# Windowed attention and a routed FFN on one core: the order of work within a pass of the first half is changed

## What is computed

```python
scores = einsum('bhts,...', q, k) * scale          # q, k, v = split(x @ W_attn + b_attn)
scores = where(causal & (j >= i - 64), scores, -inf)
x = layernorm(x + softmax(scores) @ v @ W_proj + b_proj)
expert = argmax(softmax(x @ Wr.T))                  # one of 8 for each row
y = gelu(x @ W1[expert] + b1[expert]) @ Wo + bo + x
out = layernorm(x + layernorm(y) * gamma + beta)
```

## Time and profile before

| | us |
|---|---|
| three timed runs | 616.62, 617.55, 620.0 (median 617.55) |
| the profiled execution, its own time | 610.88 |
| its span, first to last instruction | 609.0 |
| first half, about | 0 to 360 of the span |

### The profile page before, as it was taken

One profiled execution on the slowest core, in us unless ns is written; L12 is line 12 of the kernel. 1 busy time (PEld: TensorE's weight loads), 2 busy tenths in 40 slices (PEclk: granted clock), 3 DMA queues, 4 the chain that ended last, 5 costly groups with the idle time before them and its releaser, 6 DMA issues. The chain is left out here.

```text
span 609.0 us, 29717 instructions
## 1 busy us (share of the span) xinstructions
PE 525.7 (86%) x11019; PEld 446.3 (73%) x11019; DVE 444.0 (73%) x1229; ACT 374.5 (62%) x843; POOL 311.3 (51%) x570
## 2 busy tenths in 40 slices
PE   3589889898899999989997843999999999999990
PEld 2557667777677777768776632999999999998870
DVE  4336776787777778777878867678888898886543
ACT  2875755767576675746576631776667666675450
POOL 7501333343434444343434541388888888886433
PEclk9958988999999999998999985999999999999986
DMA  7695976686576667674668102133322222221100
GB/s 192 156 213 141 232 226 175 169 205 167 145 192 192 174 169 190 168 198 129 185 153 212 64 21 60 46 90 98 98 80 72 81 72 72 72 81 47 32 9 6
DMA packets 94908, 77.46 MB, mean 127 GB/s; under 512 B 37030, under 2 KB 88367, under 8 KB 94770
## 3 DMA queue, kind: packets, MB, share of 16 engines
q1 hardware_dynamic: 91410, 67.12, 42.4%
q0 software_dynamic: 3264, 8.41, 3.9%
q10 hardware_dynamic: 96, 0.04, 0.0%
HBM read 43.63 MB, written 23.62 MB: 110 GB/s over the span
## 5 line engine op out<-in xcount | busy, mean ns | idle before, releaser
L1384 PE MATMUL ps<-v_even,w_hi 128*128 128x128 f16 (+1 forms) x1280 | 170.5, 216 | 1.5 <-DVE qs L1081 0.6
L1384 PE MATMUL ps<-v_even,w_lo 128*128 128x128 f16 (+1 forms) x640 | 132.1, 215 | 0.1
L838 ACT ACTIVATE probs<-ps,b1T 128x128 f32<-128x128 f32 (+1 forms) x320 | 87.3, 361 | 72.0 <-PE ps L1384 44.0
L1366 PE MATMUL ps<-wo_hi,ks 128*128 128x256 f16 x576 | 129.2, 274 | 1.0 <-DVE ks L1074 1.0
L1384 PEld LDWEIGHTS ps<-v_even,w_hi 128*128 x1280 | 120.8, 99 | 6.2 <-issue 2.8
L886 DVE TENSOR_REDUCE mx<-ps 128x4 bf16<-128x512 f32 x128 | 82.3, 684 | 2.4 <-PE ps L1171 2.0
L666 POOL CAST attT_hi<-att 128x256 f16<-128x256 f32 x32 | 12.7, 396 | 134.9 <-DVE att L955 134.9
L739 ACT ACTIVATE qs<-ps 32x1024 f16<-32x1024 bf16 x64 | 61.3, 1004 | 30.7 <-PE ps L1259 30.7
L1366 PE MATMUL ps<-wo_lo,ks 128*128 128x256 f16 x288 | 78.9, 274 | 0.0
L733 ACT ACTIVATE probs<-ps 128x512 f32<-128x512 f32 x128 | 73.7, 610 | 4.9 <-PE ps L1193 4.2
L1074 DVE TENSOR_TENSOR ks<-probs,ks 128x512 f16<-128x512 f32 x72 | 61.5, 855 | 19.2 <-ACT ks L845 19.2
(11 more groups left out here) (221 smaller groups left out, 1341.7 us busy)
## 6 DMA issues: line engine op xcount, KB each, us to landing
qk_s<-qk_hi SPq DMA_DIRECT2D x64, 128.0 KB
w_in<-in_L_ffn_W_dram SPq DMA_DIRECT2D x32, 256.0 KB, 4.9
v_odd<-slots SPq DMA_DIRECT2D x64, 128.0 KB, 2.1
qs<-qk_s SPq DMA_DIRECT2D x16, 384.0 KB
ks<-qk_s SPq DMA_DIRECT2D x16, 384.0 KB
v_even<-v_odd SPq DMA_DIRECT2D x63, 96.0 KB, 2.6
ks<-qk_s SPq DMA_DIRECT2D x32, 144.0 KB
qk_s<-qk_lo SPq DMA_DIRECT2D x32, 128.0 KB
```

What stands on the lines that cost most here:

```text
L838: last = nc.scalar.activation(g[1 - p][:, ic, n * width:(n + 1) * width], ps_h[1 - p][:, half, col + n * width:col + (n + 1) * width], ACT ...
L1366: ins = mm(ps_y[p], h[p][hs][:, ic, :], wo[ws][:, ic, :], start=n == 0, stop=n == 3 * IC - 1)
L1384: up_ins = mm(ps_h[1 - p][:, half, col + m * width:col + (m + 1) * width], weights(ws, owners[m], k, ic), sT[1 - p][ss][:, k, at], start=k ...
```

## The change

Only the order is changed, in the first half, and one small PSUM tile moves.

- ScalarE: the copy of the inverses (`rdenT`, L790) goes between `maxima_rows(0)` and `maxima_rows(1)`; `exps(1)` goes behind the high part of q and k.
- TensorE: q and k are now (0, 1), the inverses, (2, 3), all ahead of `scores_t`. The ranks go between `scores_t` 1 and 2. `values(0)` goes between `scores` 0 and 1.
- VectorE: `att` goes ahead of the low part of W1, place and slot ahead of the low part of q and k.
- SP: the W1 load goes behind the x load and is that of the next tile (n = it + 1). It waits for `w1l_done` of tile it-1, which VectorE gives in pass `it`.
- `ps_rank` goes from bank 7 to bank 1; waits follow it (`place_done` now ahead of the projection, `v_out` and `lx_done` ahead of the ranks).

```diff
-        ps_rank = ps[:, 7, C:C + 2 * E].rearrange("p (a e) -> p a e", a=2)
+        ps_rank = ps[:, 1, 320:320 + 2 * E].rearrange("p (a e) -> p a e", a=2)
@@ SP
-                n = it
-                if a_tile(n):
-                    cols = slice(n % 2 * I // 2, (n % 2 + 1) * I // 2)
-                    wait(sp, w1l_done, n - 1)
-                    sp.dma_start(w1_in[:, cols], w1_units[n // 2][:, cols]).then_inc(w1_ld[n % 2], 16)
                 n = it + LEAD + 2
...
                     sp.dma_start(xin[n % XRING], x_rows[n]).then_inc(xin_ld[n % 3], 16)
+                n = it + 1
+                if a_tile(n):
+                    cols = slice(n % 2 * I // 2, (n % 2 + 1) * I // 2)
+                    wait(sp, w1l_done, n - 1)
+                    sp.dma_start(w1_in[:, cols], w1_units[n // 2][:, cols]).then_inc(w1_ld[n % 2], 16)
@@ ScalarE
                     maxima_rows(0)
-                    maxima_rows(1)
-                if cur:
-                    exps(0)
                 n = it - 1
                 if a_tile(n):
...
                     nc.scalar.activation(rdenT[:, :, :], ps_rden, ACT.Copy).then_inc(rdenT_out, 1)
                 if cur:
-                    exps(1)
+                    maxima_rows(1)
+                    exps(0)
...
+                if cur:
+                    exps(1)
                 if a_tile(old):
                     act.wait_ge(y_done, old + 1)
@@ VectorE
                 if a_tile(done):
+                    dve.wait_ge(rdenT_out, done + 1)
+                    wait(dve, al_done, done)
+                    nc.vector.tensor_tensor(att[:, :, :], ps_num, rdenT[:, :, :], ALU.mult).then_inc(att_done, 1)
+                if a_tile(done):
                     piece, cols = done // 2, slice(done % 2 * I // 2, (done % 2 + 1) * I // 2)
...
+                if a_tile(new):      # behind place and slot
+                    dve.wait_ge(qkh_done, new + 1)
@@ TensorE
                 scores(0)
+                values(0)
                 scores(1)
-                values(0)
                 if a_tile(old):
...
+                    wait(pe, place_done, old)
...
-                queries_keys((0, 1, 2))
+                queries_keys((0, 1))
                 if a_tile(done):
                     pe.wait_ge(rdenp_done, done + 1)
-                    wait(pe, place_done, old)
...
-                if it < 0:
-                    queries_keys((3,))
+                queries_keys((2, 3))
...
                 scores_t(1)
-                if it >= 0:
-                    queries_keys((3,))
+                if a_tile(old):
+                    pe.wait_ge(onehot_done, old + 1)
+                    pe.wait_ge(v_out, upto(it + 1))
+                    pe.wait_ge(lx_done, upto(it + 1))
+                    mm(ps_rank[:, 0, :], before[:, :], onehot[:, :], start=True, stop=True)
+                    mm(ps_rank[:, 1, :], ones_b[:, :], onehot[:, :], start=True, stop=True).then_inc(rank_done, 1)
                 scores_t(2)
                 scores_t(3)
```

More of the change, by code:

```diff
@@ L951, in _ @@
                         .then_inc(w1l_done, 1)
[L952 to L963, removed]
                 if a_tile(old):
@@ L976, in _ @@
                     nc.vector.tensor_reduce(slot_of[old % 2][:, :], placed[:, :], AX.X, ALU.max).then_inc(slot_done, 1)
+                if a_tile(new):
+                    dve.wait_ge(qkh_done, new + 1)
+                    wait(dve, qk_st[new // 2 % 2], 16 * QK_STORES * (new // 4))
+                    hi, lo = (qk[new // 2 % 2][s][:, :, :, new % 2 * P:new % 2 * P + P].rearrange("p w m t -> p (w m) t")
+                              for s in range(2))
+                    nc.vector.scalar_tensor_tensor(lo, ps_qk(new).rearrange("p w m t -> p (w m) t"), W_DOWN, hi,
+                                                   ALU.mult, ALU.subtract)\
+                        .then_inc(qkl_done, 1)
                 if it == FIRST + 1:
```

## The result

| | before | after |
|---|---|---|
| median of 20 runs each, same chip (us) | 616.68 | 619.32 |
| lowest to highest | 609.88 to 620.94 | 612.57 to 623.5 |
| profiled execution, its span | 609.0 | 614.7 |

The ratio is 1.0066, with a 95% interval of 1.0039 to 1.0093. The forecast was 610.0, with a range that ended at 617.5. On another chip the changed kernel, unaltered (after_again), came out at 0.9975 (0.993 to 1.002) of before. So "a little slower or the same" is what was measured; "7.6 us faster" is not.

A forecast was written before the change was run, and what follows sets the result against it. TensorE's start-to-start work, 8.69 us a pass, plus waits was taken to bound it. Passes 7 to 27 net -9.3, 28 to 31 +1.7, 0 to 6 nothing: -7.6 from the median 617.55 gives 610.0, range 600 to 617.5.

The forecast's parts named there:

- W1's wait goes: ScalarE's `w_hi`: W1 lands some 6 us before it, so no pass waits (11 waits, 23.0 us in the profile).
- The projection's wait goes: TensorE's projection: `attT_lo` is ready 1.2 us before it is wanted, removing a wait of 0.28 us per pass.
- The longer way, +0.67: Mark to `scores(0)`: ScalarE waits for the inverses between the maxima rows, so 4.07 us instead of 3.40.
- TensorE's own 5.29 + 0.10: `scores(0)` to the next mark: 5.29 us unhindered, plus 0.10 for one more change of matmul shape.
- VectorE with 0.4 to spare: VectorE begins `maxima(0)` 0.5 us earlier and reaches the mark with about 0.4 to spare, removing 0.3 of lateness.
- Bad passes vanish: Passes 7 to 27: 9.46 us each instead of 9.94 on average, 10.1 gained, net -9.3 after Wo's 0.8.
- The tail, 35.6: Passes 28 to 31: 35.6 us instead of 34.3, at 9.1 each and about 8.3 the last; +1.7 with the drain.
- Passes 1 to 6 at nothing: Early passes: the longer way costs 6 x 0.19 us, two W1 waits give back about as much; 0.
- The base: The 9.94 us average period from one profiled execution, and the median 617.55 from which 7.6 was subtracted.
- Longer still, a pass of 9.75, 616: Rival: `scores(1)` waits for `exps(1)` or shape changes cost 0.15 each; 1.3 us gained, 616; chance 0.16.
- Stacks as the bound: Rival: W1 loads and SP's wait delay the stacked loads, a pair of passes takes 20.4 us; +7, 625; chance 0.08.
- Nothing takes the waits' place: Rival: waiting for inverses doesn't lengthen the way, a pass takes 8.5 us; -31, 586; half of it or more, chance 0.14.

The follow-up runs named there:

- turn_early: The changed kernel with the turn of x ahead of `values(1)` instead of behind it; 616.48 us, ratio 0.9962 to before.
- w1_inv: Before with the W1 load a pass ahead and ScalarE's copy of the inverses between the two maxima rows, exponentials behind; 629.27 us, ratio 1.0158.
- inv_behind: The changed kernel with ScalarE's copy of the inverses behind both maxima rows; 610.06 us, ratio 0.9846 to before.
- tail_filled: The changed kernel with 28 useless repeated q and k matmuls in each of passes 28 to 31; 615.68 us, ratio 0.9951 to before.
- w1_only: Before with only the W1 load moved, a pass ahead and behind the x load; 609.81 us, ratio 0.9852 to before.

## Why the prediction was wrong, step by step

1. **W1's wait goes: right**, in after and alone. That the load ahead of the stores holds up no steady pass was right too: between marks 6 and 27 no `scores(0)` of after waits for `ks`.
2. **The projection's wait goes: right.** Its first matmul (L1135 with `wp`) has no idle time.
3. **The longer way, +0.67: mis-sized, and the main error in the steady pass.** It should have been +0.89: an unhindered mark has `scores(0)` 4.29 behind it (after_again, and turn_early in its passes of 9.55), not 4.07. Step by step, predicted and measured: last values piece to spreading 1.52, 1.53; spreading to copy 0.33, 0.37; copy to rows **0.27, 0.41**; rows to `exps(0)` 1.02, 1.03; `exps(0)` to `scores(0)` 1.04, 1.07. I took the 0.27 from the earlier trace rows, where exponentials stand behind the copy; before the rows, which are another form of instruction, it is 0.41 (237.31 to 237.72, and 238.48 to 238.89 in w1_inv). These sum to +0.23, the whole difference between 9.46 and 9.70.
4. **TensorE's own 5.29 + 0.10: right.** inv_behind shows 5.41 from `scores(0)` to the mark.
5. **VectorE with 0.4 to spare: too much, at no cost.** In after it is late by 0.14, in after_again it ends the maxima 0.26 ahead of the mark. The error would have mattered if the inverse waited for the mark. Yet it was enough to send me after the wrong engine once: step 5's row (0.56 behind `xT_hi`) is the most visible new wait, and not on the ring.
6. **Bad passes vanish: only in part.** 21 passes at 9.70 are 203.7; 206.5 and 207.5 were measured. I had allowed 0.8 for Wo's low part; the 2.8 and 3.8 that came on top of 203.7 lie mostly in passes 11 and 12 (21.2 and 22.2 us for two) and 16 (10.2, 10.3). Between marks 11 and 12 TensorE stands for 0.93 us in the middle of the spreading, for nothing that the profile shows ("issue"). What that is stays open. It isn't the order alone: inv_behind and tail_filled take 9.3 to 9.8 for these passes and have such stalls in others (1.12 us in pass 16, 1.24 in pass 25). w1_only has 4.9 us of long passes too, so the step from 9.94 to one even pass put stalls down to W1 that stayed.
7. **The tail, 35.6: mis-sized twice.** A pass without the turn and q and k is 9.33, not 9.1 (step 3 again), the last one 8.87, not 8.3; and I took full clock for granted, in a stretch in which TensorE idles for 1.9 us in each pass. 36.9 + 2.5 to 4.0.
8. **Passes 1 to 6 at nothing: near**, -1.6 between means that each spread by more than that.
9. **The base.** 9.94 a pass was from one execution, and 10.00 is the other's; the comparison gained 0.5 us for after by that. Subtracting from the median was sound. My range was too narrow on the slow side: three terms (0.24 in 21 passes, 2 to 3 us of stalls, 2.4 in the tail) were all too small and add up, and two of them, the pass and the tail, hang on the same edit.

In sum: forecast -7.6; + 5.0 (step 3, 21 x 0.24) + 2.5 (step 6, 3.3 for 0.8) + 2.4 (step 7, +4.1 measured for +1.7, both against the mean of before) - 1.6 (step 8) - 0.5 (step 9) = +0.2, beside the +0.1 that the means of the profiles show. The rest, to the +2.6 of the medians, lies ahead of mark 0 or in the scatter between chips (the same kernel had 1.0066 on one and 0.9975 on another); which of them stays open.

**The rivals.** "Longer still, a pass of 9.75, 616" was the nearest, for another reason than it gave: `scores(1)` doesn't wait for `exps(1)`. Stacks as the bound: not in the steady passes of after, but true of passes 4 and 6. "Nothing takes the waits' place" was wrong for this change, and right for its parts: 8.99 without the inverses' move. The Trainium skill (DMA: Bandwidth & Descriptors, Queues, rings and completion order) has descriptors of one issuing engine consumed in ring order; the 6.25 us that `scores(0)` waited for stacks issued behind 1 MB, and the 12 us that passes 4 to 6 gave back when one transfer of 1 MB was moved and the other cut in four, agree with it. They would agree as well with transfers that only share the bandwidth; no run tells the two apart. That W1's 256 KB ahead of the stores would tip steady passes over, as I had worked out from it for the rival, no run showed.

## What to carry to other kernels

Follow the ring of a pipelined pass (from one engine's instruction back to the same one a pass later) and not the last wait ahead of a landmark: the mark was late in after, and nothing hung on it. A copy put between two long instructions of an engine puts that engine's wait on the ring for all that is queued behind it; put it behind the last one whose time covers the wait. And try the parts of a change one by one: here one part was worth 1.5%, and another took it back.

## What the runs showed of the hardware

**The same cast takes twice as long beside VectorE.** POOL's first half of `att` (L666) takes 787 to 792 ns in all 32 tiles of after, and 396 to 398 in before. It is so in every kernel here that has `att` ahead of W1's low part (785 to 792 in seven profiles), and in none of the six profiles of kernels that don't (396 to 398). In after it runs while VectorE makes W1's low part from two tiles in SBUF:

```profile
237.72 0.43 DVE L949 TENSOR_TENSOR att<-ps,rdenT 128x256 f32<-128x256 f32 x1
238.06 0.68 DVE L953 SCALAR_TENSOR_TENSOR w_lo<-w_in,w_hi 128x512 f16<-128x512 f32 x1
```
```profile
238.21 0.79 POOL L666 CAST attT_hi<-att 128x256 f16<-128x256 f32 x1 [2.62 <-DVE att L949]
239.08 0.67 POOL L668 TENSOR_TENSOR attT_lo<-att,attT_hi 128x256 f16<-128x256 f32 x1
```

The second half takes 0.67 in both kernels. They overlap from 238.21 to 238.74. It costs nothing here: `attT_lo` is ready at 239.75, the projection starts at 241.09. The Trainium skill (SBUF — State Buffer, Who interferes with whom) says that a VectorE instruction with two inputs in SBUF and a GpSimd instruction that reads SBUF exclude each other, and that the second to come blocks until the first is done. By that the cast would run from 238.74 and end at 239.14, with its 0.40 of before; the trace has 239.00, so it agrees roughly.

**The order changes TensorE's own time.** The same instructions from `scores(0)` to `scores(2)` take 3.00 us with the turn of x (fp32) as the last of them and 2.86 with `values(1)` behind it, with no wait in either.

**The clock was halved among passes in which TensorE is busy for most of the time**: 7.2 us of 9.4 in the pass ahead of the first fall in after, with 1.9 us of idle time in two pieces (1.14 and 0.76). That such passes bring the half clock about is the tendency told above, six profiles of six against one of six, and not proven.
